# Decay sums of a state-space mixer: from selector matmuls into PSUM to broadcast DMAs into SBUF, masked by GpSimd

## What is computed

```
dA  = softplus(dt + dt_bias) * -exp(A_log)
cum = cumsum(dA) within a chunk
L   = exp(cum[i] - cum[j]) for i >= j, else 0        # decay matrix, per head
y   = ((C @ B^T) * L * dt[j]) @ x + D * x            # per head
g   = y * silu(gate);  out = rmsnorm(g) @ out_w^T
```

## Time and profile before

| | |
|---|---|
| median of 3 runs | 2147.99 us (2144.83 to 2150.49) |
| span of the profiled execution | 2145.0 us |
| PE busy | 1998.4 us, 93% |
| DVE busy | 1469.8 us, 69% |
| ACT busy | 1252.7 us, 58% |
| POOL busy | 1036.5 us, 48% |
| DMA | 70.50 MB, mean 33 GB/s |

### The profile page before, as it was taken

How to read it: one execution, slowest core, us unless ns; L and a number is a source line. 1 busy time by engine, 2 the same in 40 slices (tenths; PEclk the granted TensorE clock), 3 DMA queues, 4 the chain that set the end, 5 groups by cost and what they waited for, 6 DMA issues and landing times. The chain is left out here.

```text
span 2145.0 us, 32211 instructions
## 1 busy us (share of the span) xinstructions
PE 1998.4 (93%) x10956; PEld 1533.1 (71%) x10956; DVE 1469.8 (69%) x2060; ACT 1252.7 (58%) x2621; POOL 1036.5 (48%) x841
## 2 busy tenths in 40 slices
PE   6989997758999999999999999999999999999977
PEld 4855775536777777777777777777777777777755
DVE  5466555676677786777768766876777677678756
ACT  3221332326675776667757766775777577666733
POOL 4001001534565566466645654665566466646535
PEclk9965998879999999999999999999999999999988
DMA  3000001001101111110111111111111111111002
GB/s 99 1 1 20 2 2 30 25 27 50 35 30 42 31 40 35 38 35 31 37 37 40 35 37 36 30 40 36 37 35 32 41 31 40 32 40 35 20 1 69
DMA packets 40720, 70.50 MB, mean 33 GB/s; under 512 B 7392, under 2 KB 7520, under 8 KB 40544
## 3 DMA queue, kind: packets, MB, share of 16 engines
q1 hardware_dynamic: 39584, 68.21, 10.5%
q10 hardware_dynamic: 960, 0.05, 0.0%
HBM read 65.34 MB, written 2.88 MB: 32 GB/s over the span
## 5 line engine op out<-in xcount | busy, mean ns | idle before, releaser
L143 PE MATMUL ps<-mix_xnT_hi,mix_w_hi 128*128 128x512 f32 x1152 | 461.8, 401 | 12.0 <-DVE mix_bT L1518 7.0
L145 PE MATMUL ps<-mix_xnT_hi,mix_w_lo 128*128 128x512 f32 x1152 | 455.1, 395 | 0.0
L144 PE MATMUL ps<-mix_xnT_lo,mix_w_hi 128*128 128x512 f32 x1152 | 454.9, 395 | 0.0
L1308 POOL TENSOR_TENSOR mix_w_hi<-mix_w_raw,mix_ones 128x512 fp32r<-128x512 f32 x141 | 178.0, 1263 | 470.0 <-PE ps L145 467.2
L1518 DVE SCALAR_TENSOR_TENSOR mix_xT<-ps,mix_cur,mix_xT 128x510 f32<-128x510 f32 x378 | 280.7, 746 | 108.4 <-ACT mix_xT L1384 99.4
L1412 ACT ACTIVATE mix_decay<-mix_decay,mix_cur_ncum 128x128 f32<-128x128 f32 x1024 | 353.1, 397 | 0.0
L143 PEld LDWEIGHTS ps<-mix_xnT_hi,mix_w_hi 128*128 128x128 f32 x1152 | 217.4, 189 | 63.9 <-issue 12.8
L1551 DVE TENSOR_TENSOR mix_decay<-mix_decay,mix_cb 128x1536 f32<-128x1536 f32 x128 | 242.1, 1897 | 21.8 <-ACT mix_decay L1412 21.2
L145 PEld LDWEIGHTS ps<-mix_xnT_hi,mix_w_lo 128*128 128x128 f32 x1152 | 217.3, 189 | 50.9
L1407 ACT ACTIVATE mix_decay<-ps,mix_cur_ncum 128x128 f32<-128x128 f32 x512 | 183.6, 359 | 117.1 <-DVE mix_decay L1542 117.1
L1333 POOL TENSOR_TENSOR mix_gated<-mix_xT,mix_gated 128x512 f32<-128x512 f32 x128 | 163.8, 1279 | 182.2 <-DVE mix_xT L1640 174.1
(11 more groups left out here) (271 smaller groups left out, 3543.4 us busy)
## 6 DMA issues: line engine op xcount, KB each, us to landing
mix_w_raw<-in_w_in_stream SPq DMA_DIRECT2D x144, 256.0 KB, 2.7
mix_wo_raw<-in_w_out_T SPq DMA_DIRECT2D x64, 256.0 KB, 2.9
att_w_raw<-in_w_attn_T SPq DMA_DIRECT2D x12, 256.0 KB, 2.8
x<-in_x SPq DMA_DIRECT2D x8, 256.0 KB, 5.1
ffn_w_raw<-in_w_ffn_T SPq DMA_DIRECT2D x2, 1024.0 KB, 6.2
out_rows<-x SPq DMA_DIRECT2D x8, 256.0 KB, 2.0
att_wp_raw<-in_w_proj_T SPq DMA_DIRECT2D x4, 256.0 KB, 2.6
cum_parts<-mdt_parts SPq DMA_DIRECT2D x3, 256.0 KB, 2.0
```

The source lines that it names most:

```text
L143: pe.matmul(out, lh, rh, start=(k == 0), stop=False)
L144: pe.matmul(out, lh, rl, start=False, stop=False)
L145: last = pe.matmul(out, ll, rh, start=False, stop=(k == tiles - 1))
L1308: pool.tensor_tensor(w_hi[:, at % 2, :, :], raw, one, ALU.mult).then_inc(w_hi_done, 1)
```

## The change

A head's sums no longer go through TensorE and PSUM. `cum` is stored in DRAM in f32 (`cum_rows`), and for each head SyncE loads its row onto all 128 partitions, in the three-block form of `decay`, into a new tile `spread` with one buffer for head 0 and one for head 1 of a pair: one load of 4 x 256 numbers per partition (512 KB written) and one of 4 x 128 (256 KB). GpSimd masks the diagonal blocks in place with four selects a head. ScalarE's exps read `spread` and write `decay`.

The loads and masks of pair k + 1 are issued in pair k. The load for head `a` waits until ScalarE has read that buffer for pair k (`exped`). The selector matmuls, the selector, the bf16 splits and the Vector engine's minima go. The wait for y of the pair before (`y_done`), which was the Vector engine's, is now ScalarE's. The program's DMA scratch in SBUF is set to 4096 bytes.

```diff
-                dve.tensor_copy(parts[:, 0, :], cum[:, :]).then_inc(split, 1)
...
+                sp.wait_ge(step, STEPS)
+                sp.dma_start(cum_rows, cum[:, :]).then_inc(moved, 16)
...
+        spread = sb("spread", [P, 2, B, BLK])
...
@@ SyncE
+            def load_spread(g, k, a):
+
+                head = GHEADS * g + 2 * k + a
+                at_least(sp, exped, head - 1)
+                row = cum_rows[bass.ds(head, 1), :].broadcast_to([P, ROWS]).rearrange("p (b t) -> p b t", t=T)
+                sp.dma_start(spread[:, a, :, 0:T], row).then_inc(spread_in[a], 16)
+                sp.dma_start(spread[:, a, :, T:BLK], row[:, :, P:T]).then_inc(spread_in[a], 16)
...
                 for k in range(PAIRS):
-                    for dg, j in w[2 * k:2 * k + 2]:
+                    more = not (last and k == PAIRS - 1)
+                    mine = w[2 * k:2 * k + 2]
+                    for dg, j in mine[:1]:
+                        load_w(LEAD + len(NEXT) * (g + dg) + j, LEAD + j)
+                    if more:
+                        load_spread(g, k + 1, 0)
+                    for dg, j in mine[1:]:
                         load_w(LEAD + len(NEXT) * (g + dg) + j, LEAD + j)
                     load_wo(g, k)
+                    if more:
+                        load_spread(g, k + 1, 1)
@@ GpSimd
+            def causal(g, k, a):
+
+                for b in range(B):
+                    diag = spread[:, a, b, 0:T].rearrange("p (i c) -> p i c", c=P)
+                    last = pool.affine_select(out=diag, in_=diag, compare_op=ALU.is_ge, fill=MASKED, base=0,
+                                              pattern=[[0, 2], [1, P]], channel_multiplier=-1)
+                last.then_inc(selected, 1)
...
+                    if more:
+                        pool.wait_ge(spread_in[0], 32 * (PAIRS * g + k + 2))
                     wo_low(g, k)
+                    if more:
+                        causal(g, k + 1, 0)
                     for dg, j in mine[1:]:
                         split_ahead(g, dg, j)
+                    if more:
+                        pool.wait_ge(spread_in[1], 32 * (PAIRS * g + k + 2))
                     gate_pair(g, k)
+                    if more:
+                        causal(g, k + 1, 1)
@@ ScalarE
+                    at_least(act, y_done, 2 * (PAIRS * g + k))
                 for b in batches:
...
+                    for i in range(3):
+                        cols = slice(i * P, (i + 1) * P)
+                        last = act.activation(decay[:, a, b, cols], spread[:, a, b, cols], ACT.Exp,
+                                              bias=cur_ncum[:, 2 * b + i % 2, hc:hc + 1])
```

More of the change, by code:

```diff
@@ L989, in build_mixer @@
         w_stream, wo_stream = ins["w_in_stream"], ins["w_out_T"]
-        cum_parts = nc.dram_tensor("cum_parts", (3, MH, ROWS), BF16, kind="Internal").ap()
+        cum_rows = nc.dram_tensor("cum_rows", (MH, ROWS), F32, kind="Internal").ap()
         xnT_hi = sb("xnT_hi", [P, KT, ROWS], F32R)
@@ L1028, in build_mixer @@
             dt, da, cum, ones = (isb(n, [MH, ROWS]) for n in ("dt", "da", "cum", "ones"))
-            parts = isb("parts", [MH, 3, ROWS], BF16)
             made, w_in, c_in, w_done = sem("dt_made"), sem("dt_w_in"), sem("dt_c_in"), sem("dt_w_done")
-            proj, step, ex, split, moved = (sem("dt_proj"), sem("dt_step"), sem("dt_exp"), sem("dt_split"),
-                                            sem("dt_moved"))
+            proj, step, ex, moved = sem("dt_proj"), sem("dt_step"), sem("dt_exp"), sem("dt_moved")
             turned = sem("dt_turned")
+            STEPS = 17
             block = inner.enter_context(nc.Block())
@@ L1047, in _ @@
                 sp.wait_ge(c_in, 5 * 16)
[L1048 to L1051, removed]
+                sp.wait_ge(step, STEPS)
+                sp.dma_start(cum_rows, cum[:, :]).then_inc(moved, 16)
+                sp.wait_ge(moved, 16)
             @block.gpsimd
@@ L1065, in _ @@
                     lead_split(pool, n)
[L1066 to L1070, removed]
             @block.scalar
@@ L1199, in build_mixer @@
         wo_scaled, wo_hi_done, wo_lo_done = sem("wo_scaled"), sem("wo_hi_done"), sem("wo_lo_done")
-        cum_arrived = sem("cum_arrived")
+        spread_in = [sem(f"spread_in{a}") for a in range(2)]
         ones_made, cur_ready = sem("ones_made"), sem("cur_ready")
@@ L1203, in build_mixer @@
         silu_x, silu_g = sem("silu_conv"), sem("silu_gate")
-        spread, exped, selected, mixed, y_done = (sem("spread"), sem("exped"), sem("selected"), sem("mixed"),
-                                                  sem("y_done"))
+        exped, selected, mixed, y_done = sem("exped"), sem("selected"), sem("mixed"), sem("y_done")
         aux, aux_free, u_read = sem("aux"), sem("aux_free"), sem("u_read")
@@ L1277, in load_wo @@
                     .then_inc(wo_arrived[k % 2], 16)
+            def load_spread(g, k, a):
[4 more added lines that the diff above has]
+                sp.dma_start(spread[:, a, :, T:BLK], row[:, :, P:T]).then_inc(spread_in[a], 16)
             def body(g, first, last):
[L1281 to L1284, removed]
+                if first:
+                    load_spread(g, 0, 0)
+                    load_spread(g, 0, 1)
                 w = ahead(last)
                 for k in range(PAIRS):
-                    for dg, j in w[2 * k:2 * k + 2]:
+                    more = not (last and k == PAIRS - 1)
[5 more added lines that the diff above has]
+                    for dg, j in mine[1:]:
                         load_w(LEAD + len(NEXT) * (g + dg) + j, LEAD + j)
                     load_wo(g, k)
+                    if more:
+                        load_spread(g, k + 1, 1)
                 for dg, j in w[2 * PAIRS:]:
@@ L1350, in group_rstd @@
                     .then_inc(rstd_done, 1)
+            def causal(g, k, a):
[4 more added lines that the diff above has]
+                last.then_inc(selected, 1)
             def body(g, first, last):
                 w = ahead(last)
+                if first:
+                    for a in range(2):
+                        pool.wait_ge(spread_in[a], 32)
+                        causal(g, 0, a)
                 for k in range(PAIRS):
+                    more = not (last and k == PAIRS - 1)
                     mine = w[2 * k:2 * k + 2]
@@ L1533, in cur_w @@
                 return cur[:, c * MK:(c + 1) * MK]
[L1535 to L1546, removed]
             def mix(g, k, a):
@@ L1607, in body @@
                     pair = PAIRS * g + k
-                    causal(g, k, 0, first)
                     if k:
@@ L1686, in next_product @@
                 before[0] = ("gate", n_gate(g, item[1])) if item[0] == "g" else ("conv", n_conv(g, item))
[L1688 to L1701, removed]
             def turn_x(uses, conv, buf):
@@ L1792, in body @@
                         out_with(g, k, (0,), first)
-                    spread_cum(g, k, 1, first)
                     if k:
```

28 lines of the change are left out of this document (2 added, 26 removed).

## The result

| | median, us | runs | ratio to before (95% interval) |
|---|---|---|---|
| before | 2146.5 | 2144.8 to 2150.5 (4) | |
| changed | 2366.3 | 2358.0 to 2374.4 (4) | 1.102 (1.099 to 1.106) |

Slower by 220 us, where some 96 had been forecast (2240 against a profiled execution of 2145). The profiled execution of the changed kernel spans 2368.1 us.

The account below looks back on a forecast made before the run. TensorE bound the kernel before; afterwards a serial chain through the w_out load makes an ordinary pair 24.35 against 22.59 us. 46 x 1.76 = 81, +3, group ends +10, start +2: +96 on 2145, written 2240; range 2130 to 2330.

Parts of the forecast that it names:

- The bound before: TensorE's instruction stream in the mixer sets the 22.59 us pair; two selector matmul groups removed are worth 1.26 a pair.
- What lies off the path: GpSimd's eight selects, 0.46 us each, 3.7 a pair; ScalarE's exps from SBUF, 0.045 more each: GpSimd not the bound.
- The w_out load behind the spread load: On SyncE's in-order queue the w_out load now waits for head 0's exps, making a new serial path to head 1's exps.
- L = 6.5: Time from T to the landing of the w_out tile, taken as the middle of several estimates, in us.
- the forecast's case: L from 5.5 to 7.8 us, total 2175 to 2320, chance 0.66.
- y at 3.63: Term of the new pair's chain: the y matmuls on TensorE take 3.63 us, as before the change.
- The rest of the chain: Other terms of the 24.35 us pair: y's end to T, scaling and exps, product 1.79, 0.1 to TensorE, allowance 0.2.
- T: The moment in a pair when ScalarE's exps of the next pair's first head end.
- Group ends: Seven steps over a group's end into pair 0: +1.4 us each, between -0.5 and 2.5, +10 in all.
- Steps into pair 1: Steps into pair 1 of a group: 24.35 against 24.40 us, no change, but the very first +3.
- the two on the faster side: Fast transfers, L about 5, some 2140 us, chance 0.14; or the full TensorE gain, 2064 us, chance 0.06.
- The slow transfers (2400): Rival: spread loads at 200 GB/s or below, L = 8.3, second one late for gating, period 27.3 us; chance 0.14.

Follow-up runs that it names:

- the order alone: The changed kernel with SyncE issuing the w_out load of pair k before the spread load of pair k+1, head 0: 2066.6 us, ratio 0.963 to the kernel before.

## Why the prediction was wrong in its size

- **The bound before**: right. TensorE's stream set the pace, and 1.26 us a pair were in the selector groups: with the w_out load in front, most ordinary steps are 21.33 to the hundredth. That the profiled execution fits as well (2062.7 us, 2064 worked out) is partly luck: the seven steps over a group's end became only 0.6 shorter each, not 1.26, and the first pair's y came 13 us earlier, which the sum did not have.
- **What lies off the path**: right. Selects 0.43 us (0.46 worked out), exps from SBUF 0.30 apart (3.60 for 12), neither on the bound.
- **The w_out load behind the spread load** (the serial path): right, by the page's 343.7 us of ScalarE waiting for that DMA, and by the order alone undoing it.
- **L = 6.5**: 7.13, inside the 5.5 to 7.8 of the forecast's case, so +0.63. Its parts were further off than its total: SyncE's issues cost 0.37 with 0.2 between them, not 0.67 (the w_out issue came at 1.8, not 2.1), bytes cost a third or less of what I gave them, and one spread load more in front costs 0.7 beside its issue and bytes, which I had at nothing. The pair of 22.9 that the prediction names for L = 5.2 is a slip: its own sum gives 23.05.
- **y at 3.63**: this is the step that failed. It was 4.99, +1.36 a pair, because the clock falls in the idle time that L makes. The prediction named the case in its last sentence (an eighth of the pair idle, the clock could fall, on top) and gave it no price, though it had worked out that TensorE would idle some 3 us before each y. With half the clock for y, 3.63 would have been up to 7.3; a bound of 0 to 3.6 a pair belonged into the sum and the range. Ordinary steps, group ends and steps into pair 1 together, the slower y is some 87 of the 127 us by which the forecast of +96 fell short of the 223 in the profiled executions. Without it, by this estimate, the total is about 2280, inside the range. It also made the steps uneven, 24.8 to 28.1, where an even row was forecast.
- **The rest of the chain**: end of y to T 7.22 (7.10 worked out), scaling and exps 4.90 (5.03), product 1.99 (1.79 and the allowance of 0.2), to TensorE 0.07 (0.1). Together -0.04. So 24.35 + 0.63 + 1.36 - 0.04 = 26.30, against 26.29 measured.
- **Group ends**: +4.6, not +1.4, beyond the bound of 2.5. The y in front of it took 5.48 instead of 3.63 (+1.85), the chain from T to y is 14.0 instead of 11.7 (+2.3), and T comes 24.2 after y's end, not earlier than before (23.7) but later: the mask was gone, yet the exps there wait for `cur_ncum` (13.2 us in all in the page's first row above). It is so with the w_out load in front too (24.1), so L isn't the cause; which one it is was not followed up. Steps into pair 1: +1.9, not 0. Together some 35 us.
- **Rivals**: of the two on the faster side, none came. The slow transfers (2400) gave a total near the measured one, but by another cause: no transfer was slow by its bytes. GpSimd did wait for the second spread load before its gating, in 15 of the 63 pairs that have one, 39.9 us in all, 3.1 at the most; but from y's end to T the chain is 7.22, against 7.11 with the w_out load in front, so by this comparison it added some 0.1 a pair at the most.

The range ended at 2330, since it took in L's bounds and none for the clock: the clock's price in y, put at nothing, is the step that failed.

## What to carry to other kernels

When a transfer is added to an in-order queue, look at what stands behind it: a load that waited for nothing inherits the wait of the one in front, and if its reader sits between that wait's release and the end of the chain, a serial path is made; issue the old load first. And when a sum says that TensorE will idle for microseconds in every round, price the work behind the idle time at both clock levels, not at the busy one.

## What the runs showed of the hardware that was not expected

- A load in front on SyncE's queue cost the one behind it more than issue and bytes: 1.52 us for a spread load of 256 KB left out, 1.29 for two joined into one with every byte kept, of which 0.57 is issue in each; 576 KB and 768 pieces taken away within the same loads gave only 0.54.
- The Vector engine's product and a GpSimd operation that reads SBUF hold each other up, here for most of an instruction. In the changed kernel the product started at 1115.52 and ended at 1117.47; the weight split that started inside it took 2.67 us instead of 1.30, ending 1.13 after the product:

```profile
1115.93 2.67 POOL L1304 TENSOR_TENSOR mix_w_lo<-mix_w_raw,mix_w_hi 128x512 fp32r<-128x512 f32 x1
```

  The Trainium skill (SBUF — State Buffer, Who interferes with whom) says that the later of the two blocks fully; this row agrees within 0.2 us, since 1.13 and the 1.30 of the whole split differ by that. Before, this split didn't meet the product: GpSimd, not held back by the w_out tile, idled 3.06 us for TensorE there.
